# Value products of the last attention in three passes of split halves

## The reference, cut to what matters

```python
attn = jnp.einsum('bhnd,bhsd->bhns', q, k) * scale
attn = jnp.clip(attn, -11.0, 11.0)
attn = jax.nn.softmax(attn, axis=-1)
out = jnp.einsum('bhns,bhsd->bhnd', attn, v)
return out.transpose(0, 2, 1, 3).reshape(b, n, INNER) @ Wo + bo
...
x = x + jnp.tanh(g_xattn[3]) * _L3_xattn_ref(_layernorm(x), ctx_1024, ...)
x = x + jnp.tanh(g_ffn[3]) * _L3_ffn_ref(_layernorm(x), ...)
```

## Time and profile before

| what | value |
| --- | --- |
| median of 3 runs | 818.83 us (813.92 to 820.01) |
| profiled execution, own time | 816.85 us |
| its span (first to last instruction) | 815.1 us |
| PE busy | 743.7 us (91%) |
| DVE busy | 562.0 us (69%) |
| ACT busy | 431.9 us (53%) |
| POOL busy | 344.8 us (42%) |
| stage 6, tiles 4 to 15 | 578.75 to 673.50 us of the span |

### The profile page before, as it was taken

One profiled execution on the slowest core, in us unless ns is written; L12 is line 12 of the kernel. 1 busy time (PEld: TensorE's weight loads), 2 busy tenths in 40 slices (PEclk: granted clock), 3 DMA queues, 4 the chain that ended last, 5 costly groups with the idle time before them and its releaser, 6 DMA issues.

```text
span 815.1 us, 14591 instructions
## 1 busy us (share of the span) xinstructions
PE 743.7 (91%) x4533; PEld 594.3 (73%) x4536; DVE 562.0 (69%) x1644; ACT 431.9 (53%) x1175; POOL 344.8 (42%) x342
## 2 busy tenths in 40 slices
PE   6989999978899899699989879989999999999996
PEld 5647778864467667499978656747888876599984
DVE  2689878779997676567637867776657666855535
ACT  2488788858645733145553533445564244245542
POOL 1027988923111757425551011346442444324550
PEclk9999999999899969899999978999999999999999
DMA  8639950050001012356429000001000141334328
GB/s 277 124 117 385 326 166 1 22 185 1 1 1 40 1 53 92 118 182 227 133 84 332 31 1 1 1 1 40 1 1 1 53 156 53 104 112 150 124 81 314
DMA packets 55611, 83.40 MB, mean 102 GB/s; under 512 B 14816, under 2 KB 44512, under 8 KB 55264
## 3 DMA queue, kind: packets, MB, share of 16 engines
q1 hardware_dynamic: 48624, 63.52, 24.5%
q0 software_dynamic: 6912, 18.95, 6.5%
HBM read 61.41 MB, written 37.95 MB: 122 GB/s over the span
## 4 chain that ended last, share of the span: by engine, by line
PE 64%; DVE 12%; ACT 6%; issue 5%; POOL 4%; DMA 4%; DVEq 3%; SPq 1%; POOLq 0%; ACTq 0%
PE sh L853 17%; PE ob L853 15%; PE pt L810 6%; PE sh L1330 6%; PE ob L1330 6%; POOL xg L699 4%; PE pt L853 2%; PE sh L1349 2%; PE ob L1146 2%; PE pt L1322 2%; DMA work<-xg 2%; PE ob L1491 2%; DVE x L2523 1%; PE sh L903 1%; DVE hmax L2797 1%
## 5 line engine op out<-in xcount | busy, mean ns | idle before, releaser
L853 PE MATMUL ob<-area,work 128*128 128x256 f32 x512 | 116.1, 380 | 3.2 <-ACT work L1565 2.1
L708 POOL DMA_INDIRECT yt<-xn,work x72 | 69.2, 961 | 100.1 <-ACT xn L1891 83.9
L853 PEld LDWEIGHTS ob<-area,work 128*128 128x128 f32 x512 | 96.4, 190 | 19.7 <-issue 5.5
L610 POOL TENSOR_TENSOR rstd<-var,minush 128x4 f32<-128x4 f32 (+1 forms) x29 | 31.8, 1100 | 173.3 <-DVE var L2047 163.5
L1588 ACT ACTIVATE work<-work,mx 128x64 f32<-128x64 f32 x256 | 85.2, 336 | 18.0 <-DVE mx L2162 17.9
L699 POOL DMA_INDIRECT xg<-area,dest x64 | 63.7, 995 | 46.3 <-DVE dest L2500 28.7
L810 PE MATMUL pt<-ident,work 128*128 128x128 f32 (+1 forms) x292 | 40.7, 278 | 17.9 <-DMA cols<-in_L_xattn_ln_c_b 5.1
L810 PEld LDWEIGHTS pt<-ident,work 128*128 128x128 f32 (+1 forms) x292 | 32.3, 139 | 26.8 <-issue 15.8
L853 PE MATMUL ob<-area 128*128 128x256 f32 (+1 forms) x152 | 41.9, 432 | 9.2 <-DVE x L2097 5.4
L1565 ACT COPY work<-pt 128x512 f32<-128x512 f32 (+1 forms) x74 | 39.9, 582 | 17.6 <-PE pt L810 17.6
L1588 ACT ACTIVATION_READ_ACCUMULATOR work<-work,mx 128x1 f32 x256 | 48.4, 189 | 0.0
(11 more groups left out here) (363 smaller groups left out, 1887.6 us busy)
## 6 DMA issues: line engine op xcount, KB each, us to landing
work<-xg SPq DMA_DIRECT2D x80, 129.0 KB, 2.2
area<-in_L_ffn_w SPq DMA_DIRECT2D x4, 2048.0 KB, 10.7
area<-yt SPq DMA_DIRECT2D x16, 512.0 KB, 7.4
area<-in_L_xattn_Wq SPq DMA_DIRECT2D x2, 1024.0 KB, 9.8
x<-in_x SPq DMA_DIRECT2D x1, 2048.0 KB, 15.5
area<-in_L_xattn_Wo SPq DMA_DIRECT2D x2, 1024.0 KB, 11.1
area<-in_L_xattn_Wkv SPq DMA_DIRECT2D x2, 1024.0 KB, 6.3
out<-x SPq DMA_DIRECT2D x4, 512.0 KB, 4.4
```

The lines of the kernel that those rows point to most:

```text
L610: pool.tensor_tensor(rstd[:, n], var[:, n], minush[:, n], ALU.pow).then_inc(given, 1)
L708: pool.indirect_dma_start(yt[:, :], bass.IndirectOffsetOnAxis(ap=back_to[:, 2 * i + q:2 * i + q + 1], axis=0), ypair[i][:, q * D:(q + 1) * ...
L853: mm = pe.matmul(o, a, b, start=(k == 0), stop=(k == len(lhs) - 1))
```

## The change

For blocks 1 to 3 (tiles 4 to 15) the value product runs as 24 fp32r products instead of 8 in fp32: probabilities high x values high, high x values low, low x values high. The parts:

- ACT's two moves of a tile write fp32r (`probT_hi`, at the place of `probT`). A new `low(i)` on DVE subtracts that from `pt` in two halves into `probT_lo`, with a wait for the move of each half. It stands behind `add(i-1)` and ahead of `norm_stats` and `normalise(i+1)`.
- PE waits for both low halves behind the scores of t + 2 and ahead of the routing work behind the tile.
- A new `values_upper(u)` on ACT (passes 2, 6 and 10, behind the moves) copies the values of block u to fp32r in two instructions. A new `values_rest(u)` on POOL makes their low halves in place, in eight instructions of 128 x 256, placed behind `x6_rest(u)`.
- `work` moves to another address range, since its second half is now also fp32r. `sgw` gets memory of its own, and the table `upto` is made ahead of `table` rather than in `start_routing` (`up_to`; stages 3 and 7).

```diff
+            def values_rest(u):
+                pool.wait_ge(vals_hi, u)
+                if u == 1:
+                    pool.wait_ge(fold_done, 1)
+                for m in range(MI):
+                    ins = pool.tensor_tensor(values_lo(u, m), values_of(u)[:, m, :], values_hi(u)[m // 4][:, m % 4, :].bitcast(F32),
+                                             ALU.subtract)
+                ins.then_inc(vals_split, 1)
             pool.wait_ge(prob_ready[6], 1)
             keys6_rest(1)
             raw_rest(0)
             raw_rest(1)
             x6_rest(1)
+            values_rest(1)
             raw_rest(2)
             raw_rest(3)
             keys6_rest(2)
             block_rstd(7 * NB, 0)
             x6_rest(2)
+            values_rest(2)
             keys6_rest(3)
             for b in range(1, NB):
                 block_rstd(7 * NB + b, b)
                 if b == 1:
                     x6_rest(3)
+                    values_rest(3)
                 if b < 3:
                     send(7, b - 1)
...
                         if stage == 6:
+                            if b.u >= 1:
+                                pe.wait_ge(prob_low, 2 * (t - TB + 1))
                             route(behind.get(t, ()))
...
+                        if stage == 6 and b.u >= 1:
+                            pe.wait_ge(vals_split, b.u)
+                            m3 = [m for m in range(MI) for _ in range(3)]
+                            hi, lo = values_hi(b.u), [values_lo(b.u, m) for m in range(MI)]
+                            product(ob[slot][:, 0:D], [(probT_hi, probT_hi, probT_lo)[q % 3][:, m * P:(m + 1) * P] for q, m in enumerate(m3)],
+                                    [lo[m] if q % 3 == 1 else hi[m // 4][:, m % 4, :] for q, m in enumerate(m3)]).then_inc(o_full, 1)
+                            continue
...
+                def values_upper(u):
+                    act.wait_ge(sh_full, Block(u - 1).fill("sh", 6, 3)[0] + 1)
+                    for k in range(KD):
+                        a = act.copy(values_hi(u)[k], values_of(u)[:, 4 * k:4 * k + 4, :])
+                    a.then_inc(vals_hi, 1)
...
-                            move(n, n % 2, probT[:, half * 512:(half + 1) * 512])
+                            move(n, n % 2, (probT if b.u == 0 else probT_hi)[:, half * 512:(half + 1) * 512])
...
+                        if j == 2 and b.u + 1 < NB:
+                            values_upper(b.u + 1)
...
+                def low(i):
+                    for half in range(2):
+                        n, q = prob_fill(6, i, half), slice(half * 512, (half + 1) * 512)
+                        dve.wait_ge(pt_moved, n + 1)
+                        dve.tensor_tensor(probT_lo[:, q], pt[n % 2][:, :], probT_hi[:, q].bitcast(F32), ALU.subtract).then_inc(prob_low, 1)
...
                             add(pb, 6, pj, [pj])
-                            if pj == TB - 1:
-                                norm_stats(pb)
+                        if b.u >= 1:
+                            low(i)
+                        if i >= 1 and pj == TB - 1:
+                            norm_stats(pb)
                         means(i)
...
             def start_routing():
                 dve.tensor_scalar(base[:, :], iota8[:, :], float(REGION), -1.0, ALU.mult, ALU.add)
+
+            def up_to():
+
                 dve.tensor_tensor(upto[:, :, :], iota8[:, :].unsqueeze(1).broadcast_to([P, NE, NE]),
                                   iota8[:, :].unsqueeze(2).broadcast_to([P, NE, NE]), ALU.is_le)
...
+                up_to()
                 table()
```

More of the change, by code:

```diff
@@ L112, in layers_kernel @@
         mask = sb("mask", [P, NT, C], U8)
-        work = sb("work", [P, 4096])
-        with nc.sbuf_tensor("xnT", [P, 2, KD, S], F32) as xnT, nc.sbuf_tensor("area1", [P, 16384], F32) as area1, nc.sbuf_tensor("area2", [P, 12288], F32) as area2, \
+        with nc.sbuf_tensor("work", [P, 4096], F32) as work, nc.sbuf_tensor("xnT", [P, 2, KD, S], F32) as xnT, nc.sbuf_tensor("area1", [P, 16384], F32) as area1, nc.sbuf_tensor("area2", [P, 12288], F32) as area2, \
                 nc.sbuf_tensor("area3", [P, 9216], F32) as area3:
             pass
+        sb("padw", [P, 2048])
+        probR = sb("probR", [P, 2, 1024], F32R)
         xlo = sb("xlo", [P, 2, KD, S], F32R)
@@ L124, in layers_kernel @@
         sA = sb("sA", [P, 2, 512], F32R)
-        sb("pad1", [P, 1536])
+        pad1 = sb("pad1", [P, 1536], F32R)
         xnTR = sb("xnTR", [P, 2, 2, KD * S], F32R)
         sB = sb("sB", [P, 2, 512], F32R)
-        sb("pad2", [P, 512])
+        pad2 = sb("pad2", [P, 512], F32R)
         kh = sb("kh", [P, 4096], F32R)
@@ L204, in layers_kernel @@
         probT = work[:, 2048:3072]
+        probT_hi, probT_lo = (probR[:, i, :] for i in range(2))
         prob1 = [work[:, i % 2 * 1024 + i // 2 * TB * C:i % 2 * 1024 + (i // 2 + 1) * TB * C] for i in range(NB)]
@@ L220, in folded_keys, with values_of, values_lo, values_hi @@
                            ap=[list(keysA.ap[0]), [2 * H * C, KD * NB // 2], [H * C + C - 2 * j * C, 2], [1, C]])
+        def values_of(u):
+            return valsO.rearrange("p (m b d) -> p m b d", m=MI, b=NB)[:, :, u, :]
+        def values_lo(u, m):
+            o = m * NB * D + u * D
+            for first, size, a in ((0, 1024, sA[:, :, :].rearrange("p a b -> p (a b)")), (1024, 1536, pad1),
+                                   (2560, 4096, xnTR[:, :, :, :].rearrange("p a b c -> p (a b c)")),
+                                   (6656, 1024, sB[:, :, :].rearrange("p a b -> p (a b)")), (7680, 512, pad2)):
+                if first <= o < first + size:
+                    return a[:, o - first:o - first + D]
+        def values_hi(u):
+            return [key_lo[k][:, (u - 1) * 1024:u * 1024].rearrange("p (m d) -> p m d", d=D) for k in range(KD)]
         def folded_values(m, s):
@@ L290, in layers_kernel @@
         upto = wide[1][:, NE:2 * NE, :]
-        sgw = work[:, 4080:4096]
+        sgw = sb("sgw", [P, NT])
         ypair = [xn[:, i % 2 * 512:(i % 2 + 1) * 512] for i in range(NPAIR - 2)] + [work[:, i * 512:(i + 1) * 512] for i in range(2)]
@@ L374, in layers_kernel @@
         bias_split = sem("bias_split")
-        f_full, f_taken, bias_added, fold_done = map(sem, "f_full f_taken bias_added fold_done".split())
+        f_full, f_taken, bias_added, fold_done, prob_low, vals_hi, vals_split = map(
+            sem, "f_full f_taken bias_added fold_done prob_low vals_hi vals_split".split())
         q_inv, q_int, q_diag = map(sem, "q_inv q_int q_diag".split())
```

## The result

The changed kernel takes 835.47 us, median of 6 runs (830.26 to 837.12), against 817.46 for the kernel before in the same series (6 runs, 812.73 to 820.01): ratio 1.0225, 95% interval 1.0189 to 1.0262. The profiled execution took 830.26 us, its span is 828.5. The forecast of 830 had the sign, the place and the ring, but nothing for the clock and too little for `weigh` and `place` beside GpSimd. The median lies 0.47 us above the range's upper end, that of the same kernel in run 1 (833.06) inside it: on which side it falls is scatter, but the loss in the stage, 15.6 us and not 11.5, repeats.

The account below looks back on a forecast made before the run. PE set the pace in blocks 1 and 2; afterwards a DVE and ACT ring would. Ring 14.0 us against 7.1 saved, plus 4.9 of conflict, taken as +11.5 on 816.85: 828.4, in medians 830; range 821 to 835.

Parts of the forecast that it names:

- the ring: Queue loop through DVE and ACT, blocks 1 to 3: 6.78 us a plain tile against PE's 6.51; costs 14.0 us.
- the range: Whole kernel time, forecast to lie between 821 and 835 us.
- PE's product: Value product in tiles 4 to 15: 24 passes take 2.86 us instead of 3.45, saving 7.1 us in all.
- Where PE waits: PE waits for `low` at tiles 9, 14, 15: 3.1, 3.6, 1.8 us; at tile 13 for counts, 4.6.
- Prices: New subtractions in blocks 1 to 3: 0.73 us each on POOL, 0.69 on DVE, the latter without conflict waits.
- the walk: Instructions stepped through four queues from tile 2: `add(15)` comes 11.8 us later, 6.9 without DVE and POOL conflict.
- The conflict: DVE's multiplies of `normalise` wait for POOL subtractions under way; DVE loses 5.3 us, of which 4.9 arrive.
- ring without conflict: Rival: same ring in blocks 1 to 3, POOL's stretches missing the multiplies; +6.9, 825.7 us; chance 0.22.
- dearer passes: Rival: PE's passes run at the pace of their weight loads, lengthening the product; 836 us or more; chance 0.04.
- about nothing: Rival: ring and PE's saving cancel in the stage; 817 to 823 us; chance 0.10.
- PE the bound: Rival: PE still sets the pace in the stage, so its 7.1 us saving arrives; 811.7 us; chance 0.07.

Follow-up runs that it names:

- run 1: The changed kernel once more with nothing edited; 833.06 us, 1.0201 of the kernel before.
- run 4: Changed kernel with ACT's moves ahead of its exponentials in tiles 4 to 15; 823.40 us, 1.0075 of the kernel before.
- run 2: Changed kernel without VectorE's subtraction and PE's wait for it, third pass reading high probabilities; 811.04 us, 0.9941 of the kernel before.
- run 7: Changed kernel with filler matmuls where PE waits (tiles 8, 9, 11, 14, 15 and tile 12's counts); 833.79 us, 1.0228 of the kernel before.
- run 10: Changed kernel with fillers except at tile 11, GpSimd splitting values of blocks 1 and 2 only; 830.79 us, 1.0168 of the kernel before.
- run 9: Changed kernel without GpSimd's splitting of the values, with fillers except at tiles 8 and 11; 826.62 us, 1.0109 of the kernel before.
- run 3: Changed kernel without GpSimd's splitting of the values, second pass reading high values; 826.50 us, 1.0146 of the kernel before.
- run 5: Changed kernel with the old eight fp32 passes, no GpSimd splitting, VectorE's subtraction kept; 825.73 us, 1.0125 of the kernel before.
- run 8: Changed kernel with split products in block 1 alone and ACT's moves ahead of exponentials there; 817.65 us, 0.9998 of the kernel before.

## Why the prediction came out as it did

Right, by its own steps:
- **PE's product.** Forecast 2.86 us for 24 passes, measured 2.88.
- **The ring.** Forecast 6.78 us for a plain tile without conflict; the adds of tiles 4 and 5 stand at 586.62 and 593.46, 6.84 apart (6.38 in run 4, with the order turned; the next step, 7.02, is the same there, so it doesn't speak for the ring). Runs 2 and 4 show it as the cause: take the subtraction out, or the moves out from behind the exponential, and 19.7 or 11.5 us of the stage go.
- **Where PE waits.** Forecast 3.1, 4.6 (counts), 3.6 and 1.8 us at tiles 9, 13, 14 and 15; measured 3.19, 3.60, 2.24 and 1.42, the last three shorter than forecast by up to 1.4, and the waits at tiles 5, 8 and 11 not forecast.
- **Prices.** GpSimd's subtraction 0.73 us as taken; VectorE's 0.69, and neither that subtraction nor the add (0.42), which read one operand from PSUM, is stretched.

The sum of the stage was 11.8 us by the walk, 11.5 as taken, and 15.6 came. With the clock held up by fillers (run 7) it is 130.7 - 118.3 = 12.4, close to the walk. The rest by removal, one after the other: fillers 3.1, splitting of block 3 another 2.3, that of blocks 1 and 2 1.7 (runs 7, 10, 9), and 8.5 are left for the ring. The last two are off by run 9's fall of the clock: counted to the add of tile 13, ahead of that fall, the splitting of blocks 1 and 2 is worth 3.2. If the 1.6 us that run 9 loses to tile 14 are put down to the fall (an estimate, 7.23 less 5.67), the conflict is 5.5 and the ring 6.9.

The parts also depend on the order of removal. Taken out first, the splitting is worth 7.8 us (run 3), and fillers then nothing (run 9), since the wait at tile 11 comes from the stretched group behind tile 10. So:

- **The step that failed is the clock.** Every duration of PE was taken from rows at 1.00, also behind the waits that the prediction itself put there, and the sum has no term for it. The trace of before shows no fall between 580 and 673 us, where PE waits 1.10 us at most; the change makes the waits, and the falls came with them. Fillers give 3.1 us of the stage back: 1.1 at tile 9, whose wait was forecast, and 2.6 at tile 11, whose wait was not, less 0.6 lost by tile 12. This is one execution of run 7 against two alike of the changed kernel, and it is shown for the stage alone: the whole time of run 7 (1.0228 of the kernel before) is no shorter than those of the changed kernel (1.0225 and 1.0201).
- **The conflict was near in size, not in kind.** Forecast 4.9 us, all of it in multiplies; measured, with fillers, 4.0 to 5.5, of which the splitting of blocks 1 and 2 has 1.7 to 3.2 and weigh and place 2.3. Those had been counted at 1.78 us with no conflict, and the wait at tile 11, with most of what the clock cost, follows from them. The Trainium skill, "SBUF — State Buffer", section "Who interferes with whom", names copies, casts and `tensor_scalar` among the VectorE instructions that can take the shared port pair; the copy of 0.70 us agrees, and I had drawn on the half about two inputs alone. What the Trainium skill says there of one SBUF input holds outside the two-port modes of such instructions, a condition that the prediction left out.
- **The ring itself** was 6.9 in the walk and is 8.5 in run 9, 6.9 by the estimate above without that fall.

On the way from stage to whole, the median grew by 18.0 us (17.0 in run 1) for 15.6 in the stage. In other runs the two differ by -4 to +5 us, so this rest is within what the whole times scatter, and I don't explain it. With the clock counted, the forecast would have been some 3 us higher, 833.

Of the rivals, "ring without conflict" falls by run 3, "dearer passes" by run 2 and the 2.88, "about nothing" by the result. "PE the bound" was wrong here; without the subtraction (run 2) it is nearly so, with PE busy in 29.98 of 30.51 and 30.57 of 31.49 us of blocks 1 and 2, and even there 4.1 of the 7.1 us arrive.

## What to carry to other kernels

Before shortening work on the engine that bounds a stage, write down the ring of queues that the new operands pass through, in issue order, with all that stands in those queues: here 0.57 us saved in a tile was paid with a ring that waits behind an exponential it has nothing to do with. Where a forecast puts waits of 2 us and more on PE, give the sum a second value with the work behind them at the lower clock, since which waits bring a fall couldn't be told ahead, and price small VectorE instructions beside GpSimd work by GpSimd's instruction, not by their own.

## What was unexpected

- The granted clock fell to 0.50 in or behind PE's waits of 3.19, 2.27 and 3.60 us, in the repeat 3.18, 2.33 and 3.61. It isn't a matter of the wait's length alone: the wait of 2.24 at 675 brought no fall, in run 5 a wait of 3.10 at 656 us was followed by 1.00 throughout the next ten us, at tile 14 the clock fell behind 2.06 in run 9 but not behind 2.05 and 2.04 in runs 7 and 10, and in run 8 it fell after a wait of 0.77 that the kernel before passes at 1.00. What decides is open.
- A copy of 4 columns and a `tensor_scalar` of 8 last 0.70 and 0.71 us beside GpSimd subtractions of 0.73, against 0.17 and 0.23 in run 10.
- The same stretched group costs 2.3 us in one ring (runs 7 and 10) and nothing in another (run 2).
